# Attention by query tiles: one pipeline through softmax, projection, norm and router, with a tile's residual and norm statistics behind the unit's subtraction on VectorE

## What is computed

```python
x = x + xattn(ctx, ctx, layernorm(x), mask, Wv, Wk, Wq, Wo, bo)
x = x + ffn(layernorm(x), router_w, w_fc, w_proj, shared_fc, shared_proj)
# xattn: softmax(where(mask == 0, -1e20, q k^T) / sqrt(128)) v, then @ Wo.T + bo
# ffn:   relu(x @ w_fc.T)**2 @ w_proj.T; shared expert plus the top 2 of 8 experts,
#        weighted by the two router probabilities over their sum; d_ff = 512
```

## Time and profile before

| | us |
|---|---|
| median of three runs | 163.5 |
| the profiled execution | 163.0 |
| its span | 161.3 |
| first transpose of gathered rows | 89.86 |
| end of the last expert tile | 147.91 |

### The profile page before, as it was taken

The page is one execution under the profiler, slowest core; times in us unless marked ns, Lnnn a source line. Parts: engine busy times, 40 slices in busy tenths (PEclk is TensorE's granted clock), DMA queues, the critical chain, the costliest instruction groups (busy, mean ns, idle before and its releaser), DMA issues.

```text
span 161.3 us, 2858 instructions
## 1 busy us (share of the span) xinstructions
PE 136.7 (85%) x945; PEld 110.9 (69%) x945; DVE 93.0 (58%) x239; ACT 77.9 (48%) x178; POOL 93.0 (58%) x109
## 2 busy tenths in 40 slices
PE   6575869899999719988878599999999999999680
PEld 2344558667759406544357499999999999998270
DVE  1689999975966993460685554343333334361614
ACT  3299927944636514211530265555656565545500
POOL 4387927875953853007782277877876546566300
PEclk9999999999999975899999999999999999999999
DMA  5833994595000000001102978988867860020041
GB/s 122 263 140 130 256 256 135 149 285 199 13 4 0 0 0 0 0 0 36 50 21 60 298 255 296 269 256 242 275 190 229 249 206 26 10 89 19 4 131 65
DMA packets 14798, 21.08 MB, mean 131 GB/s; under 512 B 1820, under 2 KB 10402, under 8 KB 14784
## 3 DMA queue, kind: packets, MB, share of 16 engines
q1 hardware_dynamic: 12880, 18.35, 38.9%
q0 software_dynamic: 1472, 2.14, 3.9%
q10 hardware_dynamic: 432, 0.41, 0.8%
HBM read 16.20 MB, written 5.60 MB: 135 GB/s over the span
## 4 chain that ended last, share of the span: by engine, by line
PE 60%; DVE 14%; issue 8%; POOL 6%; DMA 5%; ACT 4%; DVEq 0%; POOLq 0%
PE ps L1056 17%; PE ps L1069 17%; PE ps L923 9%; POOL slots_dram L456 5%; PE ps L910 4%; DVE p_area L670 3%; DVE s_max L662 3%; PE ps L1026 2%; PE ps L1040 2%; PE ps L1016 2%; DMA small_sb<-small 2%; DMA g_area<-slots_dram 2%; DVE x_area L634 2%; PE ps L895 2%; PE ps L837 1%
## 5 line engine op out<-in xcount | busy, mean ns | idle before, releaser
L794 DVE TENSOR_TENSOR hid<-n_area 128x512 f32<-128x512 f32 x38 | 26.2, 693 | 36.4 <-ACT n_area L568 36.4
L466 POOL DMA_INDIRECT y_dram<-x_area,g_area x30 | 33.0, 1098 | 15.9 <-ACT x_area L584 11.3
L568 ACT ACTIVATE n_area<-ps 128x512 f32<-128x512 f32 x38 | 22.7, 598 | 20.1 <-PE ps L1056 16.0
L456 POOL DMA_INDIRECT slots_dram<-rows,slot x16 | 17.6, 1100 | 19.6 <-DVE slot L748 15.4
L387 POOL TENSOR_TENSOR n_area<-p_area,s_rec 128x616 f32<-128x616 f32 x16 | 19.5, 1222 | 15.5 <-DVE s_rec L683 15.1
L923 PE MATMUL ps<-p_area,v_area 128*128 128x512 f32 x40 | 20.5, 642 | 0.7 <-ACT p_area L515 0.7
L505 ACT ACTIVATE p_area<-p_area 128x616 f32<-128x616 f32 x16 | 11.5, 716 | 15.3 <-DVE p_area L670 15.3
L1056 PE MATMUL ps<-v_area,w 128*128 128x128 f32 x128 | 16.8, 276 | 0.7 <-ACT v_area L575 0.7
L1069 PE MATMUL ps<-w,hid 128*128 128x128 f32 x128 | 16.9, 275 | 0.0
L515 ACT ACTIVATE p_area<-ps 128x384 f32<-128x384 f32 (+1 forms) x32 | 12.1, 430 | 8.4 <-PE ps L910 8.3
L1056 PEld LDWEIGHTS ps<-v_area,w 128*128 128x128 f32 x128 | 15.5, 192 | 0.9 <-ACT v_area L575 0.9
(11 more groups left out here) (131 smaller groups left out, 220.9 us busy)
## 6 DMA issues: line engine op xcount, KB each, us to landing
p_area<-w_all SPq DMA_DIRECT2D x14, 512.0 KB, 4.6
w<-w_all SPq DMA_DIRECT2D x9, 512.0 KB, 4.2
slots_dram<-empty SPq DMA_DIRECT2D x2, 990.0 KB, 7.9
g_area<-slots_dram SPq DMA_DIRECT2D x6, 264.0 KB, 4.5
g_area<-y_dram SPq DMA_DIRECT2D x3, 256.0 KB, 3.9
x_area<-x SPq DMA_DIRECT2D x2, 256.0 KB, 3.2
y_dram<-x_area,g_area POOLq DMA_INDIRECT x30
g_area<-slots_dram SPq DMA_DIRECT2D x2, 198.0 KB, 4.9
```

The source lines that it names most:

```text
L456: pool.indirect_dma_start(out=slots_dram, out_offset=bass.IndirectOffsetOnAxis(ap=slot[:, b, k, t:t + 1], axis=0), in_=rows[:, b * TB + t, ...
L466: pool.indirect_dma_start(out=y_dram, out_offset=bass.IndirectOffsetOnAxis(ap=xg[:, i, ID:ID + 1].bitcast(U32), axis=0), in_=y_sb[:, i % Y ...
L568: act.activation(r[:, u % RSLOTS, :], ps[:, UP_BANK[u % UPBANKS], :], ACT.Relu).then_inc(relu_done, 1)
L794: dve.tensor_tensor(hid[:, u % HSLOTS, :], r[:, u % RSLOTS, :], r[:, u % RSLOTS, :], ALU.mult)\
```

## The change

The unit order becomes tile by tile: unit k is query tile k // 2, half k % 2, so that both halves of a tile are done two units apart, and the rest of a tile's work follows in the same loop.

- **Scores.** The float32r splits go (`three`, `kq_lo`, `xn_lo`, the 32 spreads on ScalarE, the key blocks on GpSimd). A group of four heads is one float32 product over the 32 partitions that hold these heads.
- **Softmax.** The exponential is written unnormalised, straight into the tile that is transposed. The values get a column of ones for each head, so that the product with the values also gives the sum; `probs_sum`, `probs_rec` and GpSimd's multiplication of 128x616 go. The five-piece product with the values now has the probabilities as stationary operand and 72 columns moving, for each unit.
- **A tile's chain.** On VectorE `attention_out(q)` inverts 16 sums and scales 128x128; TensorE transposes the result and projects it; `residual(q)` adds and takes the statistics, and it stands behind `scores_sub` of its unit; GpSimd's new `normalise(q)` does the power for one column and the norm with both copies of the row; TensorE transposes (`transpose_xn2`), ScalarE reads, TensorE makes the logits, VectorE takes the top two (`top_of`). All of these share the bank `MISC_BANK`, so a tile's chain starts when the one before has been read.
- **Order.** Tile q enters at k = 2q + 5. `route(0)` stands at k = 13, `ranks(0)` at k = 14, `weigh(0)` and `assign(0)` at k = 15 between maximum and subtraction. Tiles 6 and 7 run behind the loop, between pieces of the shared expert.
- **GpSimd's queue.** `normalise(0)` to `normalise(5)` stand ahead of the first transfer of rows, `normalise(6)` behind the second, `normalise(7)` behind the fourth; four transfers of batch 0 follow.
- **Start.** The sync queue no longer waits for all attention before it loads the first four spare weights of a batch.

The diff, cut to its core (QLAG is 5, VT_AT 1, RG 32, SENT_FIRST (2, 4)):

```diff
@@ GpSimd
+            def normalise(q):
+                pool.wait_ge(var2_ready, q + 1)
+                link(pool.tensor_tensor(rstd[:, 1, q:q + 1], var_eps[:, 1, q:q + 1], minus_half[:, 0:1], ALU.pow))
+                pool.tensor_scalar(rows[:, q, :, 0:D], x2[:, q, :].unsqueeze(1).broadcast_to([P, TOPK, D]),
+                                   mv[:, 1, q, 0:1], rstd[:, 1, q:q + 1], ALU.subtract, ALU.mult)\
+                    .then_inc(xn2_done, 1)
...
-            send_rows(0, 0, SENT_FIRST)
-            root_inverse(3, 1, 1)
-            send_rows(0, SENT_FIRST, TOPK * TB)
+            send_rows(0, 0, SENT_FIRST[0])
+            normalise(TB + 2)
+            send_rows(0, SENT_FIRST[0], SENT_FIRST[1])
+            normalise(TB + 3)
+            send_rows(0, SENT_FIRST[1], TOPK * TB)
@@ VectorE
+            def attention_out(q):
+                dve.wait_ge(pv_done, 2 * q + 2)
+                pv = ps[:, PV_BANK, 0:2 * VS].rearrange("p (i v) -> p i v", v=VS)
+                dve.reciprocal(sum_rec[:, :, :], pv[:, :, VH:VS]).then_inc(rec_done, 1)
+                at_least(dve, at_done, q)
+                dve.wait_ge(rec_done, q + 1)
+                dve.tensor_tensor(attn[:, :].rearrange("p (i h d) -> p i h d", i=2, d=HD),
+                                  pv[:, :, 0:VH].rearrange("p i (h d) -> p i h d", d=HD),
+                                  sum_rec[:, :, :].unsqueeze(3).broadcast_to([P, 2, UH, HD]), ALU.mult)\
+                    .then_inc(attn_done, 1)
+            def residual(q):
+                dve.wait_ge(proj_done, q + 1)
+                dve.wait_ge(xbo_ready, q // TB + 1)
+                dve.tensor_tensor(x2[:, q, :], ps[:, MISC_BANK, 0:D], x_bo[:, q, :], ALU.add).then_inc(x2_done, 1)
+                dve.wait_ge(x2_done, q + 1)
+                link(dve.bn_stats(stats[:, 1, q, :], x2[:, q, :]))
+                link(dve.bn_aggr(mv[:, 1, q, :], stats[:, 1, q, :]))
+                dve.tensor_scalar(var_eps[:, 1, q:q + 1], mv[:, 1, q, 1:2], EPS, None, ALU.add).then_inc(var2_ready, 1)
...
+            for k in range(NU):
+                q = (k - QLAG) // 2
+                if k == TB * 2 + QLAG + 2:
+                    dve.wait_ge(rank_done, 1)
+                if k >= QLAG and k % 2 == 1:
+                    if q > 0:
+                        top_of(q - 1)
+                    if q == TB + 1:
+                        read_ranks(0)
+                    attention_out(q)
+                scores_max(k)
+                if k == TB * 2 + QLAG + 2:
+                    weigh(0)
+                    assign(0)
+                scores_sub(k)
+                if k >= QLAG and k % 2 == 1:
+                    residual(q)
+                if k == 1:
+                    dve.wait_ge(x_in[1], 16)
+                    layer_norm_stats(0, x_sb, 1)
+                if k == 3:
+                    layer_norm_apply(1, 0, x_sb, xn, 1)
+                if k == TB * 2 + QLAG:
+                    route(0)
+            nets(0)
+            for q in (NT - 2, NT - 1):
+                top_of(q - 1)
+                attention_out(q)
+                residual(q)
@@ TensorE
+                q = slice(qt * P, (qt + 1) * P)
+                for i in range(2):
+                    dims = slice((2 * half + i) * RG, (2 * half + i + 1) * RG)
+                    last = pe.matmul(heads_of(2 * (k % 2) + i), lhsT=xn_t[dims, b, q], rhs=kblk[dims, b, :, :],
+                                     start=False, stop=True)
...
+                for c in range(CH):
+                    last = pe.matmul(ps[:, PV_BANK, half * VS:(half + 1) * VS], lhsT=prob_t[:, half, c, :],
+                                     rhs=v_ones[:, b * CH + c, half, :], start=(c == 0), stop=(c == CH - 1))
...
+            for k in range(NU + 2):
+                q = (k - QLAG) // 2
+                chained = k >= QLAG
+                if k < NU:
+                    scores(k)
+                if k == 1:
+                    transpose_x(2)
+                    transpose_x(3)
+                if VT_AT <= k < VT_AT + 3:
+                    transpose_v(k - VT_AT)
+                if k == VT_AT + 3:
+                    transpose_x1()
+                if chained and k % 2 == 1:
+                    transpose_attn(q)
+                if k >= 2:
+                    transpose_probs(k - 2)
+                if chained and k % 2 == 1:
+                    project_out(q)
+                if k > QLAG and k % 2 == 0:
+                    transpose_xn2(q)
+                if k >= 3:
+                    pv(k - 3)
+                if k > QLAG and k % 2 == 0:
+                    logits(q)
+                if k == TB * 2 + QLAG + 1:
+                    ranks(0)
...
+            pv(NU - 1)
+            up_shared(0, 0, 1)
+            transpose_xn2(NT - 2)
+            logits(NT - 2)
+            transpose_attn(NT - 1)
+            up_shared(0, 1, 2)
+            project_out(NT - 1)
+            up_shared(0, 2, FT)
+            transpose_xn2(NT - 1)
+            down_shared(0, 0, 1)
+            logits(NT - 1)
+            down_shared(0, 1, 3)
+            ranks(1)
             down_shared(0, 3, TB)
             transpose_group(0)
```

More of the change, by code:

```diff
@@ L31 @@
 TOPK = 2
-TLAG = 3
+QLAG = 5
+VH = UH * HD
+VS = VH + UH
+VT_AT = 1
+RG = P // JH
 PNR = 4
@@ L520, in read_attn @@
[L520 to L533 removed]
+                act.wait_ge(pt_done, k + 1)
@@ L585, in weigh @@
                                scale=xg[:, i, WT:WT + 1]).then_inc(y_read, 1)
-            for u in range(FT):
+            relu(0)
+            read_xn2(NT - 2)
+            read_attn(NT - 1)
+            for u in range(1, FT):
                 relu(u)
-            read_xn2(1)
-            copy_rows(1)
+            read_xn2(NT - 1)
             gap_exps(1)
@@ L857, in _ @@
-            pe.matmul(ps[:, PROB_BANK[1], 0:B * SK], lhsT=bd_of(1), rhs=k_t[:, :],
+            pe.wait_ge(k_read, 1)
+            pe.matmul(ps[:, KQ_BANK, 0:B * SK], lhsT=bd_of(1), rhs=k_t[:, :],
                       start=True, stop=True).then_inc(kq_done, 1)
-            def transpose_x(i, src, g, bank, done):
-                for t in range(TB):
-                    pe.wait_ge(xn_ready, TB * i + t + 1)
-                    pe.transpose(ps[:, bank, t * P:(t + 1) * P], src[:, g * TB + t, :], ident[:, :])\
-                        .then_inc(done, 1)
@@ L940, in _ @@
-            xn2 = rows[:, :, 0, 0:D]
-            def logits(b):
-                pe.wait_ge(xn2_read, b + 1)
-                for t in range(TB):
-                    last = pe.matmul(ps[:, MISC_BANK, t * NE:(t + 1) * NE],
-                                     lhsT=xn2_t[:, b, t * P:(t + 1) * P],
-                                     rhs=wo_sb[:, D:D + NE], start=True, stop=True)
-                last.then_inc(logit_done, 1)
+                    last = pe.transpose(ps[:, PROB_BANK + c // 4, c % 4 * P:(c % 4 + 1) * P],
+                                        rows_n[:, c * P:(c + 1) * P], ident[:, :])
@@ L950, in ranks, with transpose_xn2, logits @@
+            def transpose_xn2(q):
+                pe.wait_ge(xn2_done, q + 1)
+                pe.transpose(ps[:, MISC_BANK, 0:P], rows[:, q, 0, 0:D], ident[:, :]).then_inc(xt2_done, 1)
+            def logits(q):
+                pe.wait_ge(xn2_read, q + 1)
+                pe.matmul(ps[:, MISC_BANK, 0:NE], lhsT=xn2_t[:, q // TB, q % TB * P:(q % TB + 1) * P],
+                          rhs=wo_sb[:, D:D + NE], start=True, stop=True).then_inc(logit_done, 1)
             def ranks(b):
@@ L1006, in first_shared, with up_shared @@
                 return 0 if b == 0 else LAST_BLOCKS
-            def up_shared(b):
-                pe.wait_ge(xn2_read, b + 1)
-                for f in range(FT):
+            def up_shared(b, first, last):
+                pe.wait_ge(xn2_read, TB * (b + 1))
+                for f in range(first, last):
                     u = first_shared(b) + f
```

495 lines of the change are left out of this document (196 added, 299 removed).

## The result

The changed kernel takes **172.59 us** (median of 4 runs, 170.85 to 174.81) where the kernel before takes 163.13 beside it: a ratio of 1.057, interval 1.042 to 1.072. That is slower, as the larger chance had it, but 6.7 us above the predicted 165.9 and 1.1 above the range.

What follows compares the result with a forecast made beforehand. The arrival of batch 0's gathered rows, behind attention units and routing, was taken as the bound: -1.8 from the chain and +4.7 from the clock, +2.9 on 163.0, gave 165.9 us, range 158.5 to 171.5.

Steps and rivals of the forecast that it cites:

- predicted, no clock cost: The forecast's stretches without the two clock drops; the whole execution would then take 161.2 us.
- The start: Before the tiles: first maximum 2.0 us earlier, at 9.9, and tile 0 entering at 22.2 us.
- GpSimd's pair: Power and norm in each tile's chain: 0.70 + 0.60 us, 1.42 with hops, in a tile of 6.9.
- rival 1: GpSimd's power and norm bound each tile: 2.3 us, not 1.42, giving 173.0; decides from 1.54 on; chance 0.27.
- The scores: A unit's four score products and two mask products on TensorE: 1.33 us, maximum starting at 1.27.
- rival 3: Score products run side by side: 0.81 us, not 1.33, 0.25 a tile sooner, 163.9 in all; chance 0.16.
- That is what the placement buys: Residual behind the subtraction: the projection, arriving at 2.4 us, is hidden behind maximum and subtraction.
- Tail without the clock: Tiles 6 and 7, scatters and gather: normalise(7) done at 78.5, gathered rows at 88.1 us, 1.8 gained.
- The clock: Two longer TensorE idle stretches drop the clock to half pace: 2.3 + 2.4 = 4.7 us, both on the path.
- the second term: Clock loss after the 5.2 us idle ahead of the gathered rows, meeting the expert tiles: 2.4 us.
- the first: Clock loss after the 4.3 us idle ahead of normalise(5), slowing one pv, six transposes and small products: 2.3 us.

Runs made afterwards that it cites:

- e5: Changed kernel with products of zeros filling TensorE's idle places in the tail and at the start: 164.41 us, ratio 1.012 to the kernel before.
- e12: The changed kernel itself, unaltered, run once more later as a yardstick: 172.89 us, ratio 1.057 to the kernel before.
- the first profile: Profiled execution of the unaltered changed kernel in its first measurement, the longest of four: 174.81 us, span 173.1.
- e3: Changed kernel with residual and statistics moved back between maximum and subtraction: 170.52 us, ratio 1.046 to the kernel before.
- e10: Changed kernel with twelve products of zeros directly behind tile 5's second transpose: 176.88 us, ratio 1.026, on a chip where the kernel before took 170.2.
- e11: Changed kernel with three shared-expert products moved ahead of tile 5's second transpose, no zeros: 171.97 us, ratio 1.010, where the kernel before took 170.2.
- e15: Changed kernel with only eighteen products of zeros ahead of tile 5's second transpose: 166.32, 174.25, 174.28 and 175.13 us, no ratio.
- e9: e5 plus residual before subtraction, six early transfers, split norm; three shared-expert products and six zeros replace 18 zeros at tile 5's wait: 167.71 us, ratio 0.986.
- e13: e9 with nine more products of zeros ahead of the moved shared-expert products: 161.25 us, ratio 0.987 to the kernel before.

## Why the prediction was wrong, by its steps

The stretches, as spans (the execution's own time is 1.7 more):

| stretch, us | predicted, no clock cost | e5, clock full | changed kernel (e12) |
|---|---|---|---|
| tile 0's inverse | 22.2 | 21.9 | 21.8 |
| `normalise(5)` done | 65.4 | 66.6 | 66.5 |
| tile 6 | 6.4 | 7.0 | 9.0 |
| tile 7 | 6.7 | 8.3 | 11.5 |
| to the first gathered transpose | 9.6 | 9.3 | 9.4 |
| from there to the end | 71.4 | 71.4 | 74.3 |
| span | 159.5 | 162.5 | 170.6 |

- **The start: right.** First maximum 9.63 in e5 and 10.28 in the first profile for 9.9, tile 0 within 0.4 where the clock holds; the first profile lost 2.4 more there.
- **GpSimd's pair: the size was off.** 0.70 + 0.60 were 0.57 + 1.22. The norm was at its upper end, for which the prediction had its own row, 1.05 to 1.27, and I took the cheaper one. +0.55 a tile: rival 1's 2.3 was not reached, but its point of 1.54 was passed.
- **The scores: rival 3 came in part.** 1.08 for a unit, between my 1.33 and its 0.81; the maximum starts 1.02 behind the top two instead of 1.27, which is the 0.25 a tile that it named. By then VectorE has only just ended top two, inverse and scaling (39.65, maximum at 39.66), so still faster scores would not bring it sooner. The two errors, +0.55 and -0.25, offset each other in part, and 6.9 became 7.24: that the tile came out so near is luck.
- **"That is what the placement buys: set between them, the residual would wait for it": true as to the wait, false as to the gain.** The wait for the projection is 0.46 in e3, the subtraction put in its place costs 0.71. I compared having a wait with having none, not the wait with that work.
- **Tail without the clock: 3.0 too short by `normalise(7)` and the experts' start** (91.1 for 88.1). 1.2 of it is there by `normalise(5)`, 0.55 in tile 6, 1.6 in tile 7, where the power takes 0.94 and the norm 2.29, beside VectorE's squares of the shared expert, which follow each other without a gap; then -0.3. The prediction named this contention in rival 1 and gave it no term.
- **The clock: the step that failed.** 2.3 + 2.4 = 4.7 were forecast, 8.2 came. Its places were right, and so, nearly, was the second term, 2.9 for 2.4. The failed one is the first: 5.2 for 2.3. (It would be 6.3, had the norm of tile 7 taken e5's 2.29. In e12 it took 1.22: VectorE's squares lie over it there too, but they leave a gap of 0.1 just behind its start.) The term rested on "rose [...] some 6.3 us after work came again", read from one dip and carried over to other work. In the kernel before the products of `pv` ran at 512 columns ahead of that rise at 65.6; in the changed kernel the work behind the fall is `pv`s of 72 columns, transposes and short waits, and it lasted 20.5 us. Its rise at 89.0 stands in the last and longest stretch of the shared expert's 512-column products; a shorter one at 78.75 had not brought the clock back. e12 repeats the 20.5, e10 has 3.4 with 512-column products in the same place, and e5, e11 and e15 avoid the fall there. The kind of work is not the whole of it: at the start, 72-column products and transposes stood behind a fall of 3.4 us in one profile and behind one of 20.5 in another. So the size is shown, and why the clock came back so late stays open. That the start may lose the clock as well, in some executions, I did not see.
- **Sum:** 3.2 from the chain (164.4 for 161.2) and 3.5 from the clock are the 6.7 by which 165.9 was missed. So the chain alone was missed as well: with the clock held (e5) the gathered rows are transposed at 91.1, 1.3 later than in the kernel before and not 1.8 sooner.

The products ahead of the two rises of the clock, in the kernel before and then in the changed one (timelines):

```profile
62.20 3.56 PE L923 MATMUL ps<-p_area,v_area 128*128 128x512 f32 x4
```
```profile
78.75 2.01 PE L1008 MATMUL ps<-xn_t,w 128*128 128x512 f32 x2
...
85.71 3.54 PE L1008 MATMUL ps<-xn_t,w 128*128 128x512 f32 x4
```

The Trainium skill (TensorE: Matmul & The Clock Gate, HAM oscillation — how this bites in real kernels) has long waits between stretches of work throttle TensorE again, so that the next stretch starts cold. The trace agrees where TensorE waited for 4.3 us: the `pv` behind it took 2.04 instead of 1.23. The clock fell behind shorter waits too, 2.4 us in e9 and 0.5 and 0.8 at the start, and not behind 1.4 in e11. What no profile here settles is how much work of which kind brings the clock back, and why the same start lost it in two executions (e15 and the first profile) and not in e12, whose waits there were 0.1 and 0.8.

## What to carry to other kernels

An order that opens idle stretches on TensorE can lose more to the clock than it gains on the chain; look at what runs behind each stretch, and put dense work into it. Zeros beside the chain did that here; moving real work there left a hole where it had stood (e13). Judge a change to the chain with the clock held, then decide. And where an operation is moved out of a wait, set the wait against what takes its place, with both durations.

## What the runs showed of the hardware

- Behind tile 5's wait the clock stayed at half for 3.4 us with twelve 512-column products there (e10), and for 13.6 to 20.5 us in five profiles with 72-column products and transposes, though TensorE was busy for 80% and more of it by its records.
- The same program up to 40 us gave no fall in one execution (e12), one of 3.4 us in another (the first profile), and one of 20.5 us in a third (e15), in which TensorE was busy throughout by its records.
- GpSimd's norm with two per-partition scalars: 0.80 us for 128x128, 1.22 for 128x256; its power 0.57 for one column, against 1.14 for four. Beside squares that VectorE ran one behind the other the norm took 2.29 and the power 0.94; with a gap of 0.1 us between two of them just behind the norm's start it took 1.22.
- Four score products over 32 partitions each took 0.72, the time of not quite three one behind the other at 0.26 each (an estimate from the pace at 512 columns).
